# Layer 1 of a decoder on one NeuronCore: other slot order, two exponential banks in one ScalarE instruction, one maxima bank in one VectorE instruction

## The reference, cut to what matters

```
# lightning attention, 16 heads of 32, one chunk of 128 tokens per sequence
q, k, v = x @ Wq, x @ Wk, x @ Wv;  q, k = rotary(q), rotary(k)
scores = (q k^T) * dmask;          attn = scores @ v
y = rms_norm(attn, rms_w) @ Wo;    x = layernorm(x + y)
# cross attention over the 512 columns of x and of the context (8 heads of 16 rows)
qk = einsum('bhdq,bhdl->bhql', q, k) / 4
sm = softmax(qk);  ret = einsum('bhql,bhdl->bhdq', sm, v)
x = layernorm(x + gamma * ret)
```

## Time and profile before

| | |
|---|---|
| median of 3 runs | 3155.12 us (3153.93 to 3157.66) |
| profiled execution | 3162.32 us, its span 3160.5 us |
| busy share of the span | TensorE 87%, VectorE 43%, ScalarE 28%, GpSimd 19% |
| mean granted TensorE clock | 0.928 |
| layer 1's attentions | about 1164 to 2192 us of the span |

### The profile page before, as it was taken

One profiled execution on the slowest core, in us unless ns is written; L12 is line 12 of the kernel. 1 busy time (PEld: TensorE's weight loads), 2 busy tenths in 40 slices (PEclk: granted clock), 3 DMA queues, 4 the chain that ended last, 5 costly groups with the idle time before them and its releaser, 6 DMA issues. The chain is left out here.

```text
span 3160.5 us, 33789 instructions
## 1 busy us (share of the span) xinstructions
PE 2747.6 (87%) x10928; PEld 1384.0 (44%) x10990; DVE 1370.7 (43%) x2539; ACT 890.6 (28%) x1932; POOL 606.3 (19%) x634
## 2 busy tenths in 40 slices
PE   7999999999998557778778777774989999999998
PEld 3545544554554323323223233322536555665543
DVE  3545635564563423555555555560412222222245
ACT  2334434333433411234334343343001111111101
POOL 2111101110110022222122122200161111111143
PEclk9999999999999777889899899897899999999999
DMA  5111211032121023223324334223012343333144
GB/s 176 54 70 51 81 67 54 28 94 80 54 67 40 1 103 71 56 65 88 78 65 94 72 75 91 61 65 138 38 39 91 122 145 115 131 120 122 63 133 146
DMA packets 110236, 261.01 MB, mean 83 GB/s; under 512 B 21954, under 2 KB 55618, under 8 KB 98210
## 3 DMA queue, kind: packets, MB, share of 16 engines
q1 hardware_dynamic: 95202, 220.27, 23.2%
q0 software_dynamic: 13648, 38.06, 4.2%
q10 hardware_dynamic: 1264, 1.10, 0.1%
HBM read 203.76 MB, written 55.22 MB: 82 GB/s over the span
## 5 line engine op out<-in xcount | busy, mean ns | idle before, releaser
L2385 PE MATMUL d_bank<-d_w,d_xcol 128*128 x1280 | 407.5, 461 | 0.0
L1948 DVE TENSOR_REDUCE c_mx<-c_pair 128x2 f32<-128x1024 f32 x256 | 305.2, 1213 | 191.8 <-PE c_pair L1812 190.1
L1670 ACT ACTIVATE c_probs<-c_exp 128x512 f32<-128x512 f32 x512 | 277.6, 595 | 314.8 <-PE c_exp L1826 177.5
L742 PE MATMUL a_bank<-a_xT,a_ring 128*128 128x512 f32 x640 | 286.9, 600 | 11.1 <-DMA a_ident<-in_ident 11.1
L507 POOL TENSOR_TENSOR a_ry<-a_rt 128x512 f32<-128x512 f32 x80 | 128.9, 1611 | 803.3 <-DVE a_rt L994 803.3
L2385 PEld LDWEIGHTS d_bank<-d_w,d_xcol 128*128 128x128 f32 x1280 | 231.8, 191 | 102.4 <-issue 1.5
L2392 PE MATMUL d_bank<-d_w,d_hid 128*128 (+1 forms) x486 | 221.9, 592 | 0.6 <-DVE d_hid L2586 0.6
L742 PE MATMUL a_bank<-a_wo,a_ot 128*128 128x512 f32 x512 | 222.4, 592 | 0.0
L1812 PE MATMUL c_pair<-c_ks,c_qs 96*128 96x512 bf16 x512 | 154.8, 395 | 73.8 <-DVE c_r L1941 32.3
L742 PEld LDWEIGHTS a_bank<-a_xT,a_ring 128*128 128x128 f32 x640 | 120.7, 192 | 150.3 <-issue 137.0
L1826 PE MATMUL c_exp<-c_qs,c_ks 128*128 128x512 bf16 x451 | 158.8, 408 | 30.6 <-ACT c_probs L1670 12.4
(11 more groups left out here) (306 smaller groups left out, 3858.6 us busy)
## 6 DMA issues: line engine op xcount, KB each, us to landing
d_w<-in_w SPq DMA_DIRECT2D x16, 1408.0 KB, 6.6
scratch_results<-d_yrow SPq DMA_DIRECT2D x81, 256.0 KB, 2.0
a_ring<-in_wq SPq DMA_DIRECT2D x16, 1024.0 KB, 4.8
a_wo<-in_wo SPq DMA_DIRECT2D x16, 1024.0 KB, 4.9
c_ks<-scratch_kpark SPq DMA_DIRECT2D x96, 128.0 KB, 4.2
c_qs<-scratch_qpark SPq DMA_DIRECT2D x96, 128.0 KB, 4.4
d_w<-in_w SPq DMA_DIRECT2D x16, 768.0 KB, 8.4
a_ring<-in_w SPq DMA_DIRECT2D x8, 1024.0 KB, 8.4
```

The source lines that it names most:

```text
L742: ins = pe.matmul(bank[:, :], lhs(c), rhs(c), start=(c == 0), stop=(c == n - 1))
L1670: act.activation(probs[:, (LC * CH * n + k) % RING, :], bank[:, :], ACT.Exp, scale=float(CD) ** -0.5).then_inc(exped.sem, 1)
L1948: dve.tensor_reduce(mx[:, n % 2, at0:at0 + 2], bank[:, :].rearrange("p (i n) -> p i n", i=2), AX.X, ALU.max).then_inc(maxed.sem, 1)
L2385: ins = pe.matmul(bank[:, 0:FI], xcol[:, v, k, :], w13[:, bass.ds(at, 1), which, k, :].rearrange("p a n -> p (a n)"), start=(k == 0), stop ...
```

## The change

PSUM is divided anew: `one_banks` (two of 512) hold one bank of maxima scores or the transposed maxima; `exp_banks` are now two of 1024, each filled by two `second` matmuls and drained by one ScalarE instruction; the masked scores pass through the exponentials' banks; q and k pass through `step_bank`. A slot now has one `second` of two matmuls and up to three `first` of one (32 over 12 slots). The four products are split in halves over two slots. `scores` and `attend` move to the end of the phase before. `invert`, `finish` and the last `normalise` of `done` move to slots 6, 13 and 15. SyncE loads x and context after `queries` and not first. At the start, GpSimd no longer fills all of `ks` and `qs`; VectorE fills their last 32 partitions, and TensorE no longer waits for the constants before its first transposes. The fix-up of eight rows that was at the end of phase 0 is now in its slots 2 and 4.

```diff
-        pair_banks = [ctx.enter_context(nc.psum_tensor(f"c_pair{i}", [P, 1024], F32)) for i in range(2)]
-        exp_banks = [ctx.enter_context(nc.psum_tensor(f"c_exp{i}", [P, 512], F32)) for i in range(2)]
+        one_banks = [ctx.enter_context(nc.psum_tensor(f"c_one{i}", [P, 512], F32)) for i in range(2)]
+        exp_banks = [ctx.enter_context(nc.psum_tensor(f"c_exp{i}", [P, 1024], F32)) for i in range(2)]
...
-        MAX_SLOTS = 13
-        SCORES, ATTEND, TURN_X, SQUARES, OUT, V, Q, K, TURN_Q, TURN_K = 0, 2, 3, 4, 5, 7, 9, 11, 13, 14
+        MAX_SLOTS = 12
+        TURN_X, SQUARES, OUT, V, Q, K = 0, 1, 2, 4, 6, 8
+        TURN_Q, TURN_K, TURN_MAX, SCORES, ATTEND = 10, 11, 12, 13, 15
...
         def firsts(i):
-            upto = [min(2 * CH, -(-2 * CH * s // MAX_SLOTS)) for s in (i, i + 1)]
+            upto = [min(LC * CH, -(-LC * CH * s // MAX_SLOTS)) for s in (i, i + 1)]
...
             def exp_of(n, k):
-                act.activation(probs[:, (LC * CH * n + k) % RING, :], bank[:, :], ACT.Exp,
+                at0 = (LC * CH * n + 2 * k) % RING
+                act.activation(probs[:, at0:at0 + 2, :], bank[:, :].rearrange("p (i n) -> p i n", i=2), ACT.Exp,
...
             def maximum(n, k):
-                bank = pairs.wait(dve, 0, ("p", n, k))
-                dve.tensor_reduce(mx[:, n % 2, at0:at0 + 2], bank[:, :].rearrange("p (i n) -> p i n", i=2),
-                                  AX.X, ALU.max).then_inc(maxed.sem, 1)
+                bank = ones_of.wait(dve, 0, ("p", n, k))
+                dve.tensor_reduce(mx[:, n % 2, k:k + 1], bank[:, :], AX.X, ALU.max).then_inc(maxed.sem, 1)
...
+            def product(kind, n, half, rows, w, needs):
+                if half == 0:
+                    bank = steps.start(pe, 0, (kind, n), needs)
+                else:
+                    bank = steps.bank((kind, n))
+                for c in range(2 * half, 2 * half + 2):
+                    ins = pe.matmul(bank[:, :], rows[:, c, :], w[:, c, :], start=(c == 0), stop=(c == KC - 1))
+                if half:
+                    steps.done(ins)
...
-            pool.memset(ks[:], 1.0).then_inc(consts.sem, 1)
-            pool.memset(qs[:], 0.0).then_inc(consts.sem, 1)
...
-            pe.wait_ge(consts.sem, NC)
...
+            dve.memset(ks[TR:, :, :, :], 1.0).then_inc(stacks_set.sem, 1)
+            dve.memset(qs[TR:, :, :, :], 0.0).then_inc(stacks_set.sem, 1)
```

More of the change, by code:

```diff
@@ L1427, in build_layer1 @@
                 if a1 is not None:
[L1428 to L1435, removed]
+                    for kind, at in (("xt", TURN_X), ("v", V), ("q", Q), ("k", K), ("qt", TURN_Q), ("kt", TURN_K),
+                                     ("a", ATTEND)):
+                        step_order += [(kind, a1)] if i == at else []
+                    exp_order += [("s", a1, u) for u in range(2) if i == SCORES]
                 if (p, i) == FIX_TURN:
@@ L1586, in _ @@
                     queries(a2)
+                if p == 0:
+                    fix_step.wait(sp, 0, 7)
+                    sp.dma_start(t["x3"][0][0:E0, 0, :], rows[:]).then_inc(fix_out.sem, 16)
+                if seq_at(p + 4) is not None:
+                    load_x(p + 4)
+                if p > -2 and seq_at(p + 3) is not None:
+                    load_c(p + 3)
+                    load_cT(p + 3)
+                if x1 is not None:
+                    maxima(x1)
                 if done is not None:
                     store(done)
[L1589 to L1593, removed]
             stored.wait(sp, SEQS, 0)
@@ new lines, in _ @@
+                    if a2 is not None and i == TURN_X:
+                        square(a2)
+                    if a1 is not None and i == TURN_X + 1:
+                        turn_in(a1)
+                    if done is not None and i == 1:
+                        sums(done, 1)
+                    if a2 is not None and i == SQUARES + 1:
+                        rms_of(a2)
+                    if a2 is not None and i == OUT + 2:
+                        root(a2, 0)
+                    if a1 is not None and i == V + 2:
+                        values(a1)
@@ L1749, in scores @@
             def scores(n):
-                two = pairs.start_together(pe, 0, [("s", n, u) for u in range(2)], [at(turned, n, 2)])
+                two = exps.start_together(pe, 0, [("s", n, u) for u in range(2)], [at(turned, n, 2)])
                 for c in range(KC):
@@ L1757, in scores @@
                         if c == KC - 1 and r % 2:
-                            pairs.done(ins)
+                            exps.done(ins)
             def attend(n):
@@ L1781, in squares, with outputs, project @@
                 steps.done(ins)
-            def outputs(n):
-                pe.wait_ge(late.sem, 16 * NL)
-                bank = steps.start(pe, 0, ("y", n), [at(scaled, n, 1)])
-                for c in range(KC):
-                    ins = pe.matmul(bank[:, :], at_of[:, c, :], wo[:, c, :], start=(c == 0), stop=(c == KC - 1))
-                steps.done(ins)
-            def project(tiles, kind, n, w):
-                bank = tiles.start(pe, 0, (kind, n), [at(xT_ready, n, 1)])
-                if n == 0:
+            def product(kind, n, half, rows, w, needs):
[7 more added lines that the diff above has]
+                    steps.done(ins)
+            def outputs(n, half):
+                if n == 0 and half == 0:
+                    pe.wait_ge(late.sem, 16 * NL)
+                product("y", n, half, at_of, wo, [at(scaled, n, 1)])
+            def project(kind, n, half, w):
+                if n == 0 and half == 0:
                     pe.wait_ge(weights.sem, 16 * NW)
-                for c in range(KC):
-                    ins = pe.matmul(bank[:, 0:D], xT[:, c, :], w[:, c, :], start=(c == 0), stop=(c == KC - 1))
-                tiles.done(ins)
+                product(kind, n, half, xT, w, [at(xT_ready, n, 1)])
             def turn(n, i):
@@ L1929, in rotations @@
             def rotations(n, i):
-                bank = pairs.wait(dve, 0, (("q", "k")[i], n))
+                bank = steps.wait(dve, 0, (("q", "k")[i], n))
                 if n == 0 and i == 0:
```

200 lines of the change are left out of this document (91 added, 109 removed).

## The result

The changed kernel takes 3204.73 us (median of 4 runs, 3187.06 to 3210.99) beside 3155.05 for the kernel before: a ratio of 1.0147, 95% interval [1.0106, 1.0188]. It is slower by 1.5%; 3095 was forecast, with a range to 3135. The span of the profiled execution is 3209.2 us.

What follows compares the result with a forecast made beforehand. TensorE's work, waits and clock loss were taken to bound the 58.4 us phase. Gains of 26 + 10 + 6 + 4 + 7 + 8 = 61 us from the profiled 3162.3 gave 3101, less 7.2 for the median: 3095, range 3050 to 3135.

Steps and rivals of the forecast that it cites:

- start (opening): Kernel's start: transposes and first product begin earlier, v waiting for the weights; saves 6 us, between 0 and 10.6.
- phase 1: Phase from 1342.7 to 1408.6: the early fix-up brings 65.9 us to 56.0, saving 10.
- eleven full phases: From 1408.6 to 2050.7 us: each takes 56.0 instead of 58.4, 2.4 less, saving 26 us in all.
- phase 13: Phase without `a1`: no v, q, k, turns or `scores`, 41.3 us instead of 45.6, saving 4.
- phase 14: Phase with only pairs, maxima and `values`: 24.4 plus 4.8 us instead of 36.2, saving 7.
- tail: Phase 15, from the last transposed maxima to the end: 28 us instead of 36.0, saving 8.
- The walk through the full phase: One full phase priced slot by slot on TensorE: 54.8 us, 14.2 of it waits, plus 1.2 for clock, 56.0.
- Work: TensorE's matmuls in a full phase at full clock, counted from start to start: 40.6 us.
- Waits: TensorE in a full phase: one wait of 4.7 us becomes many of 0.7 to 1.75, 14.2 in all.
- Clock: Half clock behind the thin stretch T+4.0 to T+6.8 of a full phase: 0 to 2 us, 1.2 taken.
- Rival 3: Full phases: the clock falls because TensorE pauses in every slot; 63.8 us a phase, 3187 in all; chance 0.08.
- Prices: Full phase: a maximum of 512 columns 0.68 us, an exponential of 1024 columns 1.0, VectorE near 34 busy.

Runs made afterwards that it cites:

- ninth run: The changed kernel with idle matmuls in both long waits, twelve behind `scores` and eleven in slot 0: ratio 1.0027 to the kernel before.
- second run: The changed kernel with the mask ahead of `finish` on VectorE and the root of `done` one slot later: ratio 1.0011 to the kernel before.
- sixth run: The kernel before with the change's start alone (VectorE's fills replace GpSimd's, first transposes wait for no constants): ratio 0.9973 to the kernel before.
- fifth kernel: The changed kernel with the third maxima matmul at the slot's end, mask ahead of `finish`, `rms_of` ahead of the slot's exponential: ratio 0.9807 to before.
- twelfth: The kernel before with late division, new start, early fix-up, and `values` of slot 1 right behind `scores`: ratio 0.9593 to the kernel before.
- first run: The changed kernel with twelve idle matmuls behind `scores` of each full phase: ratio 1.0108 to the kernel before.

## Why the prediction was wrong

The sum by its terms, in us against the kernel before (opening: from the stage's first fill to the first turned maxima, 121.3 before):

| term | predicted | measured |
|---|---|---|
| start (opening) | -6 | -5.3 (116.0) |
| phase 0 | 0 | +1.6 |
| phase 1 | -10 | -8.5 |
| eleven full phases | -26 | +61 |
| phase 13 | -4 | +6.7 |
| phase 14 | -7 | +2.1 |
| tail | -8 | -9.2 |

The measured terms sum to 48; the spans differ by 48.7.

- **The walk through the full phase** gave 56.0 = 40.6 work + 14.2 waits + 1.2 clock. Measured is 63.9 = 43.2 busy + 15.5 idle + 5.2 clock. The two sums don't use one measure, so the terms have to be matched first.
- *Work: not shown to be off.* The walk counts from the start of one matmul to the start of the next, so the end of the matmul ahead of a wait lies inside the wait. The trace counts that end as busy. It is some 0.16 us (one 128x512 matmul takes 0.38, two take 0.60). TensorE waits at least 12 times a phase by the rows of waits above, and 18 times by the whole trace, so 2 to 3 of the 43.2 us are such ends (an estimate). That is the whole difference to 40.6.
- *Waits, some 3.9 short.* On the walk's measure they are 63.9 - 40.6 - 5.2 = 18.1 and not 14.2. The q product's wait is gone and the 0.7 waits came as walked (8.0 of `first`, 0.7 for q's rotations, 1.2 for `rms_of`). But the mask came later than walked, T+5.6 to T+7.9 (T is the turned maxima), so `second` waited 3.5 and not 2.4, and the third `first` of slot 0 waited 2.6 and not 1.2. These two, both at the end of the phase and both behind VectorE, are most of it. The waits alone would have turned a gain of 2.4 a phase into a loss of 1.5.
- *Clock, 4.0 short: the step that failed most.* "How much comes back is unknown ... I take 1.2." I had named the stretch between T+4.0 and T+6.8 and given half clock there 2 us; behind slot 0's wait I had given nothing. The clock falls in the first place in every full phase, and behind slot 0's wait for 17 us in four of the eleven, shorter in five and not at all in two. With both waits filled a phase takes 4.4 less (the ninth run) and eight of eleven run at 1.00, so it is shown that these waits bring the falls; why one wait brings a long fall, a short one or none stays open.
- **Rival 3**, at a chance of 0.08, had the direction and in part the place (the phase's end and slot 0). That its price came out (63.8 a phase beside 63.9) is luck: it added 7.8 us, all of it clock, where the clock was 4.0 over the forecast and the waits 3.9. Its mechanism, "a pause of 0.7 or more in most slots", is not what cost the time: the ninth run keeps those pauses, and in eight of eleven phases the clock stays at 1.00. What cost it are the waits for the mask (3.1 to 4.1 us) and in slot 0 (2.6). Shorter ones can do it too: in the second run TensorE waits 1.13 ahead of `scores` and 1.3 behind it, and a fall begins there in every full phase. My argument against the rival, that the clock stays up through 1.05 us, was true and beside the point. The Trainium skill ("TensorE: Matmul & The Clock Gate", the section on PSUM-queue depth-cycling) says that frequent micro-idles while banks are cycled make the clock go up and down. The runs here agree that the clock swings; of the pauses of 0.6 they show that the clock can stay up through them.
- **Phase 1**, predicted 56.0, took 57.4 without any clock loss. In its stretch no `finish` stands ahead of the mask (sequence 0's comes a phase later), the waits for the mask are 2.1 us in two pieces, and the clock stays up, although slot 0's wait of 2.62 is there too.
- **Start.** (Opening: -5.3 beside -6.) The first product came 13.4 us after the stage's first fill and not 24.4, behind `wk`, as walked. Of these 11 us the opening kept 5.3. The same start in the old order (sixth run) had 107.4: the new order gives 8.6 back in the opening, where k waits for q's rotations and `first` for maxima that nothing else covers. The old opening itself varied, 121.3 and 117.1, so the gain is 1.1 by the second of these.
- **Phases 13 and 14**, 41.3 and 29.2 predicted. Phase 13 lost to the same two waits (2.9 and 2.6), and its granted clock was 0.80. In phase 14 a new wait appears that I had not walked: with only three nearly empty slots behind the turned maxima, the next `second` comes before its transfer has landed. That it stands at the end of the chain is read from the row, not tried.

```profile
2156.82 1.04 PE L1824 MATMUL c_exp<-c_qs,c_ks 128*128 128x512 bf16 x2 [4.68 <-DMA c_qs<-c_mp]
```

- **Prices.** A maximum of 512 columns took 683 ns (0.68 taken), an exponential of 1024 1023 ns (1.0 taken), VectorE was busy 34.1 us a phase (34). By the Trainium skill ("VectorE: DVE Perf Modes", the TRN2 errata) the maximum was 0.66, an estimate: the trace agrees within 4%.

```profile
L1947 DVE TENSOR_REDUCE c_mx<-c_one 128x1 f32<-128x512 f32 x512 | 324.3, 683 | 230.0 <-PE c_one L1810 227.9
L1664 ACT ACTIVATE c_probs<-c_exp 128x1024 f32<-128x1024 f32 x256 | 260.8, 1023 | 556.4 <-PE c_exp L1824 553.0
```

What stays open: what the new division of the banks is worth by itself. At a clock of 1.00 the best phase in the new layout would be 53.1 (43.2 and the fifth kernel's 9.9; with its idle matmuls 53.9, measured), in the old it is 50.1 (the twelfth, measured). Among the waits of the fifth kernel are those of products for the single `c_step` bank (v's copy 1.3, rotations 1.0), but the order of the slots differs too, and no run separates the two.

## What to carry to other kernels

Price a chain of engines as work at full clock (read from a stretch whose granted clock is 1.00), plus waits, plus clock, and keep the three apart on both sides of the sum. Count an end of a matmul ahead of a wait either as work or as waiting, but alike in both sums. When a change replaces one long wait by several, look for the places where the longest of them stand (here at two, of 3.5 and 2.6 us), and price half clock behind each from a first trial, over many phases and not one: the same waits cost 9 us of clock in four phases here and 1.5 to 3.9 in seven. Ordering two pieces of work on the engine that it waits for (mask ahead of `finish`) was worth 4.3 us a phase. And before rebuilding the pipeline around a wait, move the work that stands in front: the late division (with the maxima sent ahead of the store) gave 2.8%, while the whole new order, which has a late division too, lost 1.5%.

## What the runs showed of the hardware that was not expected

- The same instruction stream, phase by phase, at 58.7 to 59.6 us and at 63.6 to 64.9, as the clock stayed up or fell (first run), and idle matmuls that made the kernel faster (1.0147 to 1.0027, and 0.9807 to 0.9752).
- VectorE beside GpSimd. The addition in `finish` takes 691 ns in all 16 cases before, and 692 in the fifth kernel; in the changed kernel its median is 1531:

```profile
L1971 DVE TENSOR_TENSOR c_xg<-c_xg,c_fin x16: 691/691/693, 1387.3 to 2183.4; 128x512 f32<-128x512 f32 x16
```

```profile
L1969 DVE TENSOR_TENSOR c_xg<-c_xg,c_fin x16: 692/1531/1539, 1396.4 to 2228.4; 128x512 f32<-128x512 f32 x16
```

```profile
1708.98 1.75 POOL L1612 TENSOR_TENSOR c_kp<-c_cres,c_kp 128x512 bf16<-128x512 f32 x1
```

  GpSimd works on the keys' parts from 1708.98 to 1710.73, VectorE's addition (both inputs in SBUF) runs from 1709.73 to 1711.27, and the last step of `max_parts` 1.15 instead of 0.28 just before. Both stand ahead of the mask, so that some 1.7 us of the mask's lateness may come from there (1.15 - 0.28 and 1.54 - 0.69). The Trainium skill ("SBUF — State Buffer", the section on who interferes with whom) states that a VectorE instruction with two SBUF inputs contends with a GpSimd instruction that reads SBUF; these rows agree. It was not tried by itself.
- VectorE's fill of 12288 columns of bfloat16 has a row of 10.30 us, 0.84 ns a column, where the maxima's row (1.23 us for 1024) would make it 14.8; with the second (5.18) the rows sum to 15.5 and not 22. The row may be short: the second fill waits for nothing in the program, but starts 11.53 us after the first (1163.70 and 1175.23), 0.94 ns a column, and so in each of the kernels here that have it.
